# Reciprocal products of attention's first chunks on GpSimd, and feed-forward weights loaded inside the attention stage

## The chip, the cores and the metric

One core of a Trainium2 chip runs the whole program. The time is device microseconds of one execution; the median of several is compared. The program has four stages behind one another, each with its own instruction streams for TensorE (PE), VectorE (DVE), ScalarE (ACT), GpSimd (POOL) and SyncE (SP, which issues transfers). The streams run by themselves and meet only at semaphores and at the barrier between two stages.

## The reference

```python
# x: (4, 256, 56, 56)
x = x + conv(group_norm(x))           # 7x7 pairwise self-attention convolution, softmax over 49 taps
t = tokens(x)                         # (4, 3136, 256)
n = layernorm(t)
q, k, v = heads(n @ qkv_w.T + qkv_b)  # 8 heads of 32
s = (q @ k.T * 32**-0.5 + 5) ** 2
t = t + (s / s.sum(-1)) @ v @ proj_w.T + proj_b
n = layernorm(t)
w = n @ wr + br                       # one weight per token
sel = top(w, 3136 // 2 - 1)           # 1567 tokens of each batch
y = n
y[sel] += w[sel] * (gelu(n[sel] @ w1 + b1) @ w2 + b2)   # 256 -> 1024 -> 256
t = t + y
```

## The kernel before

The first two stages (group norm, projections and the convolution) run until about 1635 us and are not touched. The third is attention, the fourth the routed feed-forward.

**Attention.** A batch is `t`, 128 partitions x 2 x 3136 (channels on partitions, tokens along the free axis), in seven chunks of 448 tokens. `EARLY` is 5. Before the loop over the batches the first five chunks of batch 0 are normalized. For each chunk VectorE adds the input and the convolution's output into `t` (`residual`, line 1880, two inputs from SBUF); ScalarE squares (`square`, 1003); GpSimd adds the two halves of the sum and of the squares (`half_sum` 1008, `half_sq` 1013); PE averages over the channels with a matrix of 1/256 (`stats`, 1016, once for the mean and once for the squares); ScalarE squares the mean (`mean2`, 1037); VectorE takes the variance (1043) and subtracts the mean into `xn` (1048); ScalarE takes the square root (`std`, 1058); VectorE takes the reciprocal (1064) and multiplies `xn` by it (`scale`, 1068). The order on VectorE is, for chunk c: variance, subtraction, reciprocal, product, and the residual of chunk c + 2. ScalarE squares the residual of chunk c + 1 before the mean of chunk c. The last of the five chunks has its reciprocal and product later, beside the keys.

Behind the five chunks VectorE copies the selector matrix `sel` (2069), PE multiplies the value bias by the output projection (`pb_mm`, 2266), VectorE adds that to `pb_s` (2071), and then the loop over the batches begins with the key projections (PE 2127) and VectorE's addition of the key bias (1911). The loop runs three times, the fourth batch has a body of its own; for batches 1 to 3 the first five chunks are normalized beside the outputs of the batch before, by `center` and `scale`.

**The last batch's outputs.** For every chunk and each of two halves PE projects (2084) into PSUM and VectorE joins it with `t` into the single output tile `tout` (1886, semaphore `t2_done`); SP stores the tile (1678, `t2_out`), and the next chunk's join waits for that. Beside this the front of the feed-forward works: token tiles of batches 0 and 1 are turned (PE 1420) and their moments taken, batch 0's tokens are normalized, searched for the selected ones, scattered to DRAM by GpSimd (1218, 25 transfers) and the selected rows loaded back packed, by GpSimd's queue (1231, 1233, into `xc0`). SP's last instructions wait for all seven chunks' stores; then comes the barrier (1449).

**Routed feed-forward.** It allocates what remains of SBUF after the attention stage's buffers are given back, among them the weights `w1_s`, `w2_s`, `b1_s` and three tiles `tb` for adding back. GpSimd first issues the three loads of weights (2416, 1 MB for each matrix, 4 KB for the bias), then clears the end of `hid` (2417) and the last rows of `xc` (2418), then normalizes every second token tile of batch 1 (1215). PE turns four packed tiles (2589), which ScalarE copies (2484) once those clears are done, and then waits for the weights (`w_in`). After that every engine follows a list of positions written out by hand (`STEPS`): 32 up products (2599) and 13 down products (2609) for each batch, with the search, turning and normalizing of the next batches and the adding back of the last between them. ScalarE takes the square root of batch 1's variances (`root`, 1279) before its first gelu (2489).

## Time and profile before

| what | value |
|---|---|
| median of 3 runs | 3521.96 us (3514.76 to 3528.95) |
| the profiled execution | 3520.25 us |
| its span | 3518.4 us |
| PE busy | 3016.6 us, 86% |
| VectorE busy | 2481.0 us, 71% |
| GpSimd busy | 2145.4 us, 61% |
| ScalarE busy | 1981.1 us, 56% |
| granted TensorE clock, mean | 0.942 of full |

The page gives for each engine the sum of its instructions' times. The timeline gives start and length of each; in brackets stands the idle time before it and what ended that. An instruction's length runs from its start to its end, standing still for a port or a queue included.

### The profile page before, as it was taken

The page shows a single profiled execution, that of the slowest core. Times are in us where ns is not written, and L with a number is a line of the kernel's source. Part 1 is how long each engine was busy: PE and PEld are TensorE (multiplying, and loading weights), DVE is VectorE, ACT ScalarE, POOL GpSimd, SP SyncE. Part 2 cuts the span into 40 slices and gives each one's busy share as a digit, 9 for nine tenths or more (in the row PEclk, how much of TensorE's full clock was granted, in tenths as well). Part 3 has the DMA queues.
Part 4 walks back from the last instruction along what each step waited for, and adds up shares of the span by engine and source line. Part 5 has one row for each costly group of instructions (what it writes and reads, how often), then busy time and mean ns, then how long its engine had stood idle before and what let it go on. Part 6 is the DMA issues. An engine that isn't in the chain of part 4 may idle for free. (4 is left out here: it accounts for less than half of the span.)

```text
span 3518.4 us, 102494 instructions
## 1 busy us (share of the span) xinstructions
PE 3016.6 (86%) x42638; PEld 1526.2 (43%) x42638; DVE 2481.0 (71%) x2173; ACT 1981.1 (56%) x3387; POOL 2145.4 (61%) x1235
## 2 busy tenths in 40 slices
PE   4988888888888887875899999999999989689997
PEld 1234434444444443432552354335334533267775
DVE  6369999999999999997763676476558655364322
ACT  1566556666655666642458656865775576434221
POOL 3369988889999888975671177037505751234433
PEclk9999899988999998988899999999999999799998
DMA  6531111221212122103011211111111122235544
GB/s 227 159 122 59 58 52 36 65 62 55 63 50 62 36 65 60 57 16 105 13 54 36 67 29 42 46 54 29 54 54 33 30 57 75 105 114 174 161 146 146
DMA packets 190699, 257.34 MB, mean 73 GB/s; under 512 B 88974, under 2 KB 151674, under 8 KB 188216
## 3 DMA queue, kind: packets, MB, share of 16 engines
q1 hardware_dynamic: 178348, 218.25, 20.6%
q0 software_dynamic: 11520, 32.55, 3.0%
q8 instruction: 357, 5.85, 0.7%
q14 instruction: 78, 0.64, 0.1%
q10 hardware_dynamic: 396, 0.05, 0.0%
HBM read 152.23 MB, written 79.27 MB: 66 GB/s over the span
## 5 line engine op out<-in xcount | busy, mean ns | idle before, releaser
L847 PE MATMUL ps<-late,ident 32*32 32x504 f32 x21952 | 1097.2, 645 | 213.8 <-issue 143.9
L689 DVE TENSOR_TENSOR late<-ps,late 128x3584 f32<-128x3584 f32 x280 | 1056.4, 3792 | 103.4 <-PE ps L847 95.0
L847 PEld LDWEIGHTS ps<-late,ident 32*32 32x32 f32 x21952 | 485.0, 108 | 471.7 <-issue 402.0
L319 POOL TENSOR_TENSOR late<-ex,late 128x1792 f32<-128x1792 f32 x140 | 530.0, 3786 | 64.0 <-PE ps L847 31.2
L1583 POOL TENSOR_TENSOR pool<-share 128x768 f32<-128x768 f32 (+1 forms) x200 | 348.3, 1748 | 182.8 <-ACT share L1779 135.7
L1825 ACT ACTIVATE phq<-ps 128x896 f32<-128x896 f32 x448 | 391.9, 920 | 72.8 <-PE ps L2177 68.7
L287 POOL TENSOR_TENSOR y<-xa 128x1568 f32<-128x1568 f32 x98 | 324.2, 3316 | 116.8 <-PE ps L823 115.8
L298 POOL TENSOR_TENSOR ex<-lg,mx 128x1568 f32<-128x1568 f32 x98 | 345.7, 3546 | 12.7 <-DVE mx L670 12.7
L2177 PE MATMUL ps<-qst,sel 96*128 96x448 bf16 x1120 | 296.3, 357 | 22.2 <-ACT phq L1825 16.4
L519 ACT ACTIVATE ps<-ex 128x448 f32<-128x448 f32 x280 | 149.4, 534 | 284.8 <-DVE late L689 284.7
L1928 DVE TENSOR_TENSOR pool<-ps,share 128x1280 f32<-128x1280 f32 (+1 forms) x200 | 295.5, 1481 | 4.0 <-ACT ps L1785 2.8
L2150 PE MATMUL ps<-pool,share 128*32 128x288 f32 (+3 forms) x3200 | 236.8, 412 | 27.5 <-ACT pool L1790 12.7
L543 ACT ACTIVATE y<-ps,u2c,s2c 128x784 f32<-128x784 f32 x189 | 189.3, 1001 | 126.0 <-PE ps L823 125.7
L818 PE MATMUL ps<-y,cw1bd 32*32 32x392 f32 x3136 | 217.1, 518 | 20.8 <-ACT y L532 9.6
L2127 PE MATMUL ps<-share,xt 128*128 128x256 f32 (+1 forms) x800 | 225.1, 406 | 6.5 <-ACT share L1786 5.5
L2177 PEld LDWEIGHTS ps<-qst,sel 96*128 96x128 bf16 x1120 | 82.8, 98 | 320.2 <-ACT phq L1825 172.8
L550 ACT ACTIVATE lg<-ps,par 128x784 f32<-128x784 f32 x196 | 179.1, 914 | 75.4 <-PE ps L834 75.2
L2046 DVE TENSOR_TENSOR at<-ps,rd 128x448 f32<-128x448 f32 x56 | 35.0, 624 | 260.1 <-PE ps L2242 238.1
L1008 POOL TENSOR_TENSOR lm20a<-t 128x448 f32<-128x448 f32 x16 | 18.2, 1138 | 325.4 <-DVE t L1880 325.4
L834 PE MATMUL ps<-y,cw2bd 32*32 32x392 f32 x3024 | 186.5, 523 | 28.1 <-ACT y L543 23.1
L655 DVE TENSOR_TENSOR run<-lg,run 128x1568 f32<-128x1568 f32 x70 | 195.6, 2794 | 2.2 <-issue 1.6
L2599 PE MATMUL ps<-xct,w_s 128*128 128x392 f32 x512 | 181.0, 499 | 11.2 <-DMA w_s<-in_w 6.8
(280 smaller groups left out, 5029.0 us busy)
## 6 DMA issues: line engine op xcount, KB each, us to landing
late<-planes SPq DMA_DIRECT2D x14, 2480.0 KB, 9.0
pf<-pf_dram SPq DMA_DIRECT2D x392, 55.1 KB
planes<-ex SPq DMA_DIRECT2D x7, 1984.0 KB, 9.4
conv_dram<-late SPq DMA_DIRECT2D x56, 224.0 KB, 4.8
t<-in_x SPq DMA_DIRECT2D x28, 448.0 KB, 4.0
xt<-conv_dram SPq DMA_DIRECT2D x28, 448.0 KB, 6.3
t_dram<-tout SPq DMA_DIRECT2D x28, 448.0 KB, 2.9
pool<-t_dram SPq DMA_DIRECT2D x24, 512.0 KB
```

Source lines behind the costliest of these rows:

```text
L287: pool.tensor_tensor(o, x1, x2, ALU.subtract).then_inc(z_ready, 1)
L298: pool.tensor_tensor(ex[:, i], lg[:, i], m, ALU.subtract).then_inc(shifted, 1)
L319: pool.tensor_tensor(o[:, :, 0:SHARE], w.unsqueeze(2).broadcast_to([P, RW, SHARE, W]), xw, ALU.mult).then_inc(own_ready, 1)
L689: v.tensor_tensor(o, w, xw, ALU.mult).then_inc(prod_ready, 1)
L818: pe.matmul(ps[at:at + 32, k + r // 2, 0:CW].rearrange("p (j w) -> p j w", w=W), diag(cw1, r), y[32 * r:32 * r + 32, :, h * W:(h + 1) * W] ...
L847: mm = pe.matmul(ps[32 * h:32 * h + 32, 4 + r, 0:DENC], diag(ident, r), x[32 * r:32 * r + 32, h].rearrange("p s w -> p (s w)"), start=begi ...
L1583: pool.tensor_tensor(phk[j % 2][0:r, :, ROT_V * DH:FLIN].rearrange("p h (r i) -> p h r i", i=DH), ki.unsqueeze(2).broadcast_to([r, HPG, RO ...
L1825: act.activation(dst, src, ACT.Square).then_inc(phq_done, 1)
L1928: v.tensor_tensor(phk[j % 2][0:r, :, DH:ROT_V * DH].rearrange("p h (r i) -> p h r i", i=DH), same.unsqueeze(2).broadcast_to([r, HPG, ROT_V ...
L2127: mm = pe.matmul(ps[0:r, 4 + j % 2, 0:HPG * DH + P], xn[:, k, j * P:j * P + r], wkv_s[:, k, hg, :], start=(k == 0), stop=(k == CH - 1))
L2150: pe.matmul(ps[DH * h:DH * h + DH, f, 0:hi - lo], kv[j % 3][0:r, v0:v0 + DH], phk[j % 2][0:r, h, lo:hi], start=(j == 0), stop=(j == NT - 1))
L2177: mm = pe.matmul(ps[:, h, 0:CT], sel[:, f, :], qst[:, h, ch(c)], start=True, stop=True)
```

## The change

`scale` is split. In the chunks before the loop VectorE does only the reciprocal (`rstd`), and a new `scale_pool` has GpSimd multiply chunk c - 1 after the half sums of chunk c; the keys wait for these products. The last reciprocal there is followed by the selector's copy and the bias addition, which now stand before the variance of chunk 4, and PE does the bias product ahead of the averages of chunk 4. `t` belongs to `Front` and stays allocated in the feed-forward stage. `w1_s` and `w2_s` lie over its first 2048 columns, and two of the three `tb` tiles behind them. GpSimd issues the three loads inside the attention stage, once ten joins of the last batch are done (chunks 0 to 4, `WEIGHTS_FROM` is 5), ahead of the loads of packed rows. The wait for the last chunk's store moves from SP at the end of attention to SP and ScalarE in the feed-forward stage.

```diff
--- before.py
+++ after.py
@@ -1057,11 +1057,21 @@
         v = self.var[c % 2][:]
         act.activation(v, v, ACT.Sqrt, bias=self.eps[:]).then_inc(self.s_std_done, 1)
 
+    def rstd(self, v, n, c):
+        v.wait_ge(self.s_std_done, n * NCT + c + 1)
+        r = self.var[c % 2]
+        v.reciprocal(r[:], r[:]).then_inc(self.s_rstd, 1)
+
+    def scale_pool(self, pool, c):
+        pool.wait_ge(self.s_rstd, c + 1)
+        pool.wait_ge(self.s_cent, c + 1)
+        o = self.xn[:, :, self.ch(c)]
+        pool.tensor_tensor(o, o, self.var[c % 2][:].unsqueeze(1).broadcast_to([P, CH, CT]), ALU.mult).then_inc(self.s_xn_done, 1)
+
     def scale(self, v, n, c):
         i = n * NCT + c
-        v.wait_ge(self.s_std_done, i + 1)
+        self.rstd(v, n, c)
         r = self.var[c % 2]
-        v.reciprocal(r[:], r[:]).then_inc(self.s_rstd, 1)
         v.wait_ge(self.s_rstd, i + 1)
         v.wait_ge(self.s_cent, i + 1)
         o = self.xn[:, :, self.ch(c)]
@@ -1091,6 +1101,7 @@
 NEXT_TOK = [21 + p for p in range(NPAIR)]
 NEXT_MOMENTS = [range(0, 0)] * 5 + [range(0, 4), range(4, 8)]
 WIDEN_AT, SPREAD_AT, ROWS_AT = 6, 12, 14
+WEIGHTS_FROM = -(-CH * HID // CT)
 TURN = ((4, 5), (7, 6))
 
 
@@ -1110,7 +1121,7 @@
 
 
 
-    def __init__(self, ctx, nc, t2_dram, wr, br, b2, tri_dram, keep):
+    def __init__(self, ctx, nc, t2_dram, wr, br, b2, tri_dram, w1, b1, w2, keep):
         def sb(name, shape, dt=F32):
             return ctx.enter_context(nc.sbuf_tensor(name, shape, dt))
 
@@ -1119,6 +1130,7 @@
 
         self.ps = keep["ps"]
         self.sources = (wr, b2, br, tri_dram)
+        self.wide_sources = (b1, w1, w2)
         first = sb("xt0", [P, NT, CW1])
         self.xt = [first]
         self.xn = first[:].rearrange("p j c -> p (j c)")[:, 0:CH * S].rearrange("p (k s) -> p k s", s=S)
@@ -1150,6 +1162,12 @@
         self.yg03 = self.share[:, (NSEL_T + NT) * CW1:(NSEL_T + NT + 1) * CW1]
         self.ident = sb("ident2", [P, P])
         self.eps = sb("eps3", [P, 1])
+        self.t = sb("t", [P, CH, S])
+        low, high = self.t[:, 0], self.t[:, 1]
+        self.w1_s = low[:, 0:CH * HID].rearrange("p (k h) -> p k h", h=HID)
+        self.w2_s = high[:, 0:HT * C].rearrange("p (h c) -> p h c", c=C)
+        self.tb = [x[:, CH * HID:CH * HID + CH * GCOL].rearrange("p (k s) -> p k s", s=GCOL) for x in (low, high)]
+        self.b1_s = sb("b1_s", [P, HT])
         self.stat = rest(NT, 6)
         self.msum, self.mdif, self.var, self.rstd, self.nbias = [rest(NT) for _ in range(5)]
         self.key, self.res, self.low, self.high = [rest(NT) for _ in range(4)]
@@ -1167,6 +1185,8 @@
         self.seq_i, self.digit_i = self.sign, self.part[:, 0, 0:BASE - 1]
 
         self.first_in = sem("first_in3")
+        self.w_in = sem("w_in3")
+        self.t2_last = sem("t2_last")
         self.ready0 = sem("ready3")
         self.t_in = [sem(f"t_in{k}") for k in range(RING)]
         self.turned = sem("turned3")
@@ -1205,6 +1225,10 @@
         pool.iota(self.seq_i[:], [[P, NT]], base=1, channel_multiplier=1).then_inc(self.ready0, 1)
         pool.iota(self.digit_i, [[1, BASE - 1]], base=1, channel_multiplier=0).then_inc(self.ready0, 1)
         pool.memset(self.ones[:], 1.0).then_inc(self.ready0, 1)
+
+    def weights(self, pool):
+        for o, src in zip((self.b1_s, self.w1_s, self.w2_s), self.wide_sources):
+            pool.dma_start(o[:], src).then_inc(self.w_in, 16)
 
     def clear(self, pool):
         pool.memset(self.zeros[:], 0.0).then_inc(self.ready0, 1)
@@ -1454,7 +1478,7 @@
             return ctx.enter_context(nc.semaphore(name))
 
         ps = keep["ps"]
-        t = sb("t", [P, CH, S])
+        t = front.t
         xn = front.xn
         qsp = front.share[:, 0:3 * S // 2].bitcast(BF16).rearrange("p (f s) -> p f s", f=3)
         shared = [3 * S // 2]
@@ -1508,7 +1532,7 @@
         ready0 = sem("ready0")
         gate = sem("gate2")
         x_in = [sem(f"x_in2{c}") for c in range(NCT)]
-        t2_out = [sem(f"t2_out{c}") for c in range(NCT)]
+        t2_out = [sem(f"t2_out{c}") for c in range(NCT - 1)] + [front.t2_last]
         tsum = sem("tsum")
         pb_mm = sem("pb_mm")
         pb_done = sem("pb_done")
@@ -1619,6 +1643,8 @@
             for c in range(EARLY):
                 norm.half_sum(pool, tsum, 0, c)
                 norm.half_sq(pool, 0, c)
+                if c > 0:
+                    norm.scale_pool(pool, c - 1)
             pool.wait_ge(ready0, 7)
             with pool.Fori(0, B - 1) as b:
                 keys(b, 0)
@@ -1643,6 +1669,8 @@
             pool.wait_ge(front.placed, 1)
             for j in range(NT):
                 front.scatter_one(pool, 0, j)
+            pool.wait_ge(t2_done, (B - 1) * NCT * CH + WEIGHTS_FROM * CH)
+            front.weights(pool)
             pool.wait_ge(qst_in, 16 * 3 * HPG * B * NCT)
             pool.wait_ge(qst_last, 16 * 3 * HPG * B)
             pool.memset(front.xc0[:, NSEL_T - 1, :], 0.0).then_inc(front.ready0, 1)
@@ -1729,7 +1757,7 @@
                 front.load(sp, 1, g)
             for c in range(4, NCT):
                 store(B - 1, c)
-            for c in range(NCT):
+            for c in range(NCT - 1):
                 sp.wait_ge(t2_out[c], 16 * B)
 
         @block.scalar
@@ -2061,15 +2089,17 @@
             for c in range(EARLY):
                 norm.center(v, 0, c)
                 if c < EARLY - 1:
-                    norm.scale(v, 0, c)
+                    norm.rstd(v, 0, c)
                 if c + 2 < EARLY:
                     residual(0, c + 2)
-            v.wait_ge(w_in, NW_IN)
-            v.wait_ge(ready0, 7)
-            v.tensor_copy(sel[:], self32).then_inc(ready0, 1)
-            v.wait_ge(pb_mm, 1)
-            v.tensor_tensor(pb_s[:], pb_s[:], ps[:, 0, 0:CH], ALU.add).then_inc(pb_done, 1)
+                if c == EARLY - 2:
+                    v.wait_ge(w_in, NW_IN)
+                    v.wait_ge(ready0, 7)
+                    v.tensor_copy(sel[:], self32).then_inc(ready0, 1)
+                    v.wait_ge(pb_mm, 1)
+                    v.tensor_tensor(pb_s[:], pb_s[:], ps[:, 0, 0:CH], ALU.add).then_inc(pb_done, 1)
             v.wait_ge(pb_done, 1)
+            v.wait_ge(norm.s_xn_done, EARLY - 1)
             with v.Fori(0, B - 1) as b:
                 body(b, True)
             body(B - 1, False)
@@ -2258,13 +2288,14 @@
 
             pe.wait_ge(avg_in, 16)
             for c in range(EARLY):
+                if c == EARLY - 1:
+                    pe.wait_ge(w_in, NW_IN)
+                    for h in range(CH):
+                        for k in range(HG):
+                            mm = pe.matmul(ps[:, 0, h:h + 1], pw_s[:, k, h * P:(h + 1) * P], bv_s[:, k:k + 1], start=(k == 0), stop=(k == HG - 1))
+                    mm.then_inc(pb_mm, 1)
                 norm.stats(pe, 0, c)
-            pe.wait_ge(w_in, NW_IN)
             pe.wait_ge(ready0, 8)
-            for h in range(CH):
-                for k in range(HG):
-                    mm = pe.matmul(ps[:, 0, h:h + 1], pw_s[:, k, h * P:(h + 1) * P], bv_s[:, k:k + 1], start=(k == 0), stop=(k == HG - 1))
-            mm.then_inc(pb_mm, 1)
             pe.wait_ge(pb_done, 1)
             with pe.Fori(0, B - 1) as b:
                 body(b, True)
@@ -2329,21 +2360,18 @@
             return ctx.enter_context(nc.semaphore(name))
 
         ps = keep["ps"]
-        front = Front(ctx, nc, t2_dram, wr, br, b2, tri_dram, keep)
+        front = Front(ctx, nc, t2_dram, wr, br, b2, tri_dram, w1, b1, w2, keep)
         rows_dram = front.rows_dram = [nc.dram_tensor(f"rows_dram{b}", (ROWS, CW1), F32, kind="Internal").ap() for b in range(B)]
         attention_block(nc, front, *keep["attention"], keep)
 
-        tb = [sb(f"tb{k}", [P, CH, GCOL]) for k in range(RING)]
+        tb = front.tb + [sb("tb2", [P, CH, GCOL])]
         xt, dest, rows, ident = front.xt, front.dest, front.rows, front.ident
         yg = [front.yg + [front.yg03]] + [[sb(f"yg{k}{i}", [P, CW1]) for i in range(GT)] for k in range(1, RING)]
         xc = [front.xc0, sb("xc1", [P, NSEL_T, CW1])]
         xct = sb("xct", [P, CH, NUP])
         hid = sb("hid6", [P, HT, NSEL_T * P])
         yt = front.yt
-        w1_s = sb("w1_s", [P, CH, HID])
-        w2_s = sb("w2_s", [P, HT, C])
-        b1_s = sb("b1_s", [P, HT])
-        w_in = sem("w_in3")
+        w1_s, w2_s, b1_s, w_in = front.w1_s, front.w2_s, front.b1_s, front.w_in
         ready0, turned, placed = front.ready0, front.turned, front.placed
         tb_in = [sem(f"tb_in{k}") for k in range(RING)]
         out_st = [sem(f"out_st{k}") for k in range(RING)]
@@ -2412,8 +2440,6 @@
                             at += 1
                         tile += k
 
-            for o, src in ((b1_s, b1), (w1_s, w1), (w2_s, w2)):
-                pool.dma_start(o[:], src).then_inc(w_in, 16)
             pool.memset(hid[:, :, NUP:NSEL_T * P], 0.0).then_inc(ready0, 1)
             pool.memset(xc[1][:, NSEL_T - 1, :], 0.0).then_inc(ready0, 1)
             for j in range(1, NT, 2):
@@ -2452,6 +2478,7 @@
                 c0, w = q * GCOL, group_cols(q)
                 sp.dma_start(out_v[b, :, :, c0:c0 + w], tb[n % RING][:, :, 0:w]).then_inc(out_st[n % RING], 16)
 
+            sp.wait_ge(front.t2_last, 16 * B)
             for b in range(B + 1):
                 for pos, (kind, m, h) in enumerate(STEPS):
                     for q in range(NG):
@@ -2494,6 +2521,7 @@
                 pack(0, m)
             front.root(act, 1)
             act.wait_ge(w_in, NW_IN)
+            act.wait_ge(front.t2_last, 16 * B)
             for b in range(B):
                 for pos, (kind, m, h) in enumerate(STEPS):
                     if kind == "up":
```

## Rows read from the trace of the kernel before

**Rows 1.** The page's busy times: engine, us, share of the span, instructions.
```profile
PE 3016.6 (86%) x42638; PEld 1526.2 (43%) x42638; DVE 2481.0 (71%) x2173; ACT 1981.1 (56%) x3387; POOL 2145.4 (61%) x1235
```

**Rows 2.** The chain of waits in order of time: start us, us, what.
```profile
3047.78 0.58 POOL b_s L2416
...
3048.88 9.89 DMA w_s<-in_w
3058.81 2.98 PE ps L2599 x4
```

**Rows 3.** Timeline, start of attention, one chunk's period: start us, us, engine, line, operation.
```profile
1666.38 0.62 DVE L1043 TENSOR_TENSOR lvar0a<-ps,lm20a 128x448 f32<-128x448 f32 x1 [1.50 <-issue]
...
1667.91 2.95 DVE L1064 RECIPROCAL lvar0a<-lvar0a 128x448 f32<-128x448 f32 x1
...
1670.89 1.09 DVE L1068 TENSOR_TENSOR xt<-xt,lvar0a 128x896 f32<-128x896 f32 x1
1671.90 1.08 DVE L1880 TENSOR_TENSOR t<-t,xt 128x896 f32<-128x896 f32 x1
...
1674.49 0.62 DVE L1043 TENSOR_TENSOR lvar1a<-ps,lm21a 128x448 f32<-128x448 f32 x1 [1.50 <-issue]
```

**Rows 4.** Timeline, the end of the first chunks.
```profile
1677.84 1.70 PE L1016 MATMUL ps<-pool,avg 128*128 128x448 f32 x2
...
1680.02 0.62 DVE L1043 TENSOR_TENSOR lvar0a<-ps,lm20a 128x448 f32<-128x448 f32 x1
1680.55 1.08 DVE L1048 TENSOR_TENSOR xt<-t,ps 128x896 f32<-128x896 f32 x1
...
1681.55 0.48 DVE L2069 CAST sel<-share 96x640 bf16<-96x640 f32 x1
...
1682.17 1.84 PE L2266 MATMUL ps<-bv_s,pw_s 128*128 128x1 f32 x8 [2.64 <-DVE sel L2069]
...
1684.45 5.48 PE L2127 MATMUL ps<-share,xt 128*128 128x256 f32 x12 [0.44 <-DVE pb_s L2071]
1686.56 0.29 DVE L1911 TENSOR_TENSOR share<-ps,share 128x128 f32<-128x128 f32 x1 [2.35 <-PE ps L2127]
```

**Rows 5.** Timeline, VectorE and GpSimd at once: convolution, then start of attention.
```profile
698.88 2.58 DVE L655 TENSOR_TENSOR run<-lg,run 128x1568 f32<-128x1568 f32 x1
699.73 1.96 POOL L320 COPY late<-ex 128x224 f32<-128x224 f32 x1
...
1646.15 1.13 POOL L1013 TENSOR_TENSOR pool<-pool 128x448 f32<-128x448 f32 x1
1646.28 1.96 DVE L1880 TENSOR_TENSOR t<-t,xt 128x896 f32<-128x896 f32 x1 [1.29 <-DMA xt<-conv_dram]
...
1697.79 1.74 POOL L1583 TENSOR_TENSOR pool<-share 128x768 f32<-128x768 f32 x1
```

**Rows 6.** Timeline, end of attention and start of the feed-forward.
```profile
3035.51 9.11 SPq L1678 DMA_DIRECT2D t_dram<-tout  x2
...
3043.54 0.68 DVE L1886 SCALAR_TENSOR_TENSOR tout<-ps,pb_s,t 128x448 f32<-128x448 f32 x1 [1.93 <-PE ps L2084]
...
3047.36 1.09 PE L2589 MATMUL ps<-ident,share 128*128 128x128 f32 x4 [3.87 <-PEq L1449]
...
3050.07 0.34 POOL L2418 MEMSET xc<- 128x257 f32 x1
...
3051.60 0.81 ACT L2484 ACTIVATE xct<-ps 128x256 f32<-128x256 f32 x2 [0.51 <-PE ps L2589]
```

**Rows 7.** Joins before the end; transfers of 3003 to 3030 (last: us to landing); a window.
```profile
3018.29 0.69 DVE L1886 SCALAR_TENSOR_TENSOR tout<-ps,pb_s,t 128x448 f32<-128x448 f32 x1 [3.11 <-PE ps L2084]
...
3028.38 0.69 DVE L1886 SCALAR_TENSOR_TENSOR tout<-ps,pb_s,t 128x448 f32<-128x448 f32 x1 [0.53 <-PE ps L2084]
...
t_dram<-tout SPq DMA_DIRECT2D x1, 448.0 KB, 2.8
...
3052.00:3059.00 7.00, 0.19 (x1) 0.19 (x2) 0.50 (x2) 0.59 (x2) 5.71 (x11) 0.50 0.87 362
```

## The prediction

> **What bounds the kernel now.** I read the page's totals first: PE is busy for 86% of the span [rows 1], so no engine idles for long and gains can only come from seams. Then the chain of waits: through the feed-forward stage it is almost all matmuls, and its first long piece is a transfer, 9.89 us of weights at 3048.88, behind three issues on GpSimd, and the first feed-forward matmul stands at 3058.81 when it lands [rows 2]. That is one seam. The other is the start of attention, read from the timeline: PE works there only in snatches, because five chunks of batch 0 are normalized one after another and VectorE carries the chain [rows 3], with the bias product after them [rows 4]. Batches 1 to 3 are normalized beside other work, and the loop's code is not touched, so the two seams are all that can move.
>
> **Part A, the first chunks. Period of a chunk.** From one variance to the next VectorE takes 1674.49 - 1666.38 = 8.11 us [rows 3]: variance and subtraction, the reciprocal (2.95, starting at 1667.91), the product (1670.89), the residual of the chunk after next (1671.90), ending 1672.98, and 1.51 us in which ScalarE squares that residual and then the mean. The change takes the product out. What it occupied is 1671.90 - 1670.89 = 1.01 us, plus the gap behind the reciprocal: the product waited for the reciprocal's own semaphore (1670.89 against an end at 1670.86), while an instruction without such a wait starts about 0.08 us before its forerunner ends (1671.90 against 1671.98). So 1.09 us a chunk go, for the three chunks 0 to 2 behind whose reciprocal a residual stands: 3.3 us.
>
> **What GpSimd does with the product.** It costs more there: 128x768 took 1.74 us [rows 5]; scaled to 128x896 that is an estimate of 2.05. GpSimd is idle at that moment, and nobody waits for these products before the keys begin. But its queue is in order: the next chunk's two half sums stand behind the product. And the two engines do not run freely side by side. A residual (two inputs from SBUF, 1.08 us elsewhere) that began at 1646.28, with GpSimd on a half product since 1646.15, took 1.96 us: it ended 0.96 us after GpSimd did. The other way round, a GpSimd copy begun at 699.73 while VectorE had run a two-input operation since 698.88 took 1.96 us and ended 0.23 after it [rows 5]. So whoever starts first keeps the other out. After the change the product (released by the reciprocal's semaphore, some 0.08 us after its end) and the residual (not waiting for it, 0.05 to 0.08 before that end) meet at every chunk. I take VectorE as first, by about 0.15 us: the residual costs its 1.08, GpSimd stands for 1.0 and multiplies for 2.05, so it is free 2.15 us after the residual, and the half sums (1.13 each) end 4.4 us after it. PE's averages need those and the subtraction before them, which ends 3.1 us after the residual; the first half sum is there at 3.3. PE starts 0.1 to 0.2 late and has 2 us to spare before the next variance. So the price on the path is nothing; if GpSimd is first, it is 2.0 us a chunk.
>
> The Trainium skill (SBUF — State Buffer, section "SBUF: two separate sides") says the same of the pair: an exclusive lock, held for the whole instruction by whichever starts first, between GpSimd and a VectorE operation with two SBUF inputs. By that rule alone either order is possible, and the second is a rival below.
>
> **The end of the prologue.** Call the last chunk-3 variance V (1674.49 now). Now: the last averages end at V + 5.05 (1677.84 + 1.70), but VectorE still multiplies, so the variance of chunk 4 starts at V + 5.53 (1680.02), its subtraction 1680.55, the copy of the selector 1681.55, then PE's bias product (1682.17, 1.84 us), its addition, the first projection at V + 9.96 (1684.45) and VectorE's first key addition at V + 12.07 (1686.56) [rows 4]. After: the bias product stands on PE ahead of the last averages, in a hole that PE has there (its chunk-3 averages end 5 us after the variance before, the period is 7.0, the product takes 1.8; the small weights have landed, DMA was idle from about 1665, some 4 us before). The reciprocal of chunk 3 ends at V + 4.48, the copy (0.48) and the addition follow, the variance of chunk 4 starts at about V + 5.25, the subtraction ends at V + 6.9; GpSimd's last product, held off by the copy if by anything, ends at V + 7.1. PE may project from V + 5.5, the first projection takes the 2.1 us that it takes now, so the first key addition starts at V + 7.6 instead of V + 12.07. That is 4.45 us. Part A: 3.3 + 4.45 = 7.75 us. If the averages or the entry of the loop are a little later, 6.5; at most 8.5.
>
> **Part B, the seam before the feed-forward.** First, the stage ends earlier. Now SP waits for the last output store: issued by 3044.62 (the second of the two from 3035.51), landed 2.3 us later, and PE starts at 3047.33 to 3047.36 [rows 6]. After, nothing waits for it at the barrier; the last to arrive is SP with its issue at 3044.62, or VectorE at 3044.22 (3043.54 + 0.68). With the same 0.45 us of barrier the stage starts at 3045.1: 2.25 us. ScalarE and SP wait for that store later, at about 3046.9, before anything they need.
>
> Second, GpSimd no longer issues three loads, 1.62 us from 3047.78 [rows 2], ahead of the two clears. ScalarE's copies of the turned rows wait for the second clear. Now clear at 3050.07, second pair of copies ending 3052.41 (3051.60 + 0.81): 2.34 us [rows 6]. After: GpSimd starts 0.45 after the stage does, clears hid (0.7), the second clear starts at 3046.2, the copies end at 3048.6. Then nothing holds the first feed-forward matmul but these copies, for the weights are there: it starts at 3048.6 instead of 3058.81, 10.2 us in all, the 2.25 among them. ScalarE's square root of the second batch's variances waits for VectorE until about 3049.1, still ahead of the first gelu (the first up product needs 3.0 us [rows 2], PE being granted half its clock there [rows 7]). What follows (gelu, normalizing, the second search) is engine work that starts behind that matmul and moves with it.
>
> **Are the weights there?** They are issued once the tenth output tile of the last batch is joined: 3018.29 + 0.68 = 3019.0 [rows 7]. Beside the tokens' loads, 3.5 MB moved in 9.9 us now, at 362 GB/s [rows 2, 7]. After, 2.1 MB of weights and then the packed rows (1.57 MB, whose issue is now behind that wait on GpSimd's queue instead of at 3004) take an estimated 10 to 12 us at such a rate and are there by 3033, with 12 us to spare. They run beside one output store, whose landing (2.8 us now) frees the single output tile for the join at 3028.38; it is issued at about 3020 and so may take 8 us. I take nothing for it; bounds -0 and +2 us.
>
> **Sum.** 7.75 + 10.2 = 17.95 us. The profiled execution took 3520.25 (span 3518.4), so 3502.3 by it. The median of the three runs is 1.7 above it: 3504.0 for a median.
>
> **Rivals.**
> (1) GpSimd takes the port first. For: the instruction that lost in [rows 5] came only 0.13 us late, and my lead for VectorE is no larger. Against: a semaphore lies between on GpSimd's side, none on VectorE's. Then the residual ends 3.1 us after the reciprocal instead of 2.1 as now; each of three chunks gets 1.0 longer instead of 1.1 shorter, and the selector's copy waits for the last product too (1.6 of the 4.45 lost): A becomes about -3 + 2.9, nothing. 10.2 us remain: 3511.8. The Trainium skill's rule on the pair, above, allows this.
> (2) The weights are early but another wait takes their place: the packed rows, the root, the second batch's normalizing on ScalarE, or the averages. Half of B's second piece gone: about 13 us gained, 3509.
> (3) Slower: the copies crowd the output stores. Place: the store of chunk 4 and the join at 3028.38, then everything behind. If 3.7 MB moved at 73 GB/s, the page's mean over the span, and ahead of the store, they would take 50 us, and the joins and with them the stage would move by X, up to 42. It decides from X = 17.95, where the store lands 26 us after 3020. At X = 36 the time is 3540. Against: 362 GB/s just there, and DMA otherwise idle from 3023 to 3036.
> (4) More: PE keeps its upper clock over the shorter pause. The first four up matmuls take 2.98 us, against 1.32 later; 1.7 to 2 us more, 3502.
>
> **Numbers.** Forecast 0.55, rival (1) 0.19, (2) 0.15, (3) 0.03, (4) 0.08. Half a per cent, about what a measurement of this kernel tells from no change (its three runs lie 0.4% apart), is 17.6 us, so the forecast lies on the boundary: slightly under half of it, (4), and some scatter of the runs make 0.42 for faster; within 0.5%, 0.55; slower 0.03. The range reaches from the forecast with its upper bounds and (4), less a scatter of the runs, 3496, to (1) with scatter, 3514.
>
> **What would show it.** The reciprocals' period on VectorE at the start: 7.0 us right, 9.1 rival (1), where the residuals would last 3 us and not 1.1. GpSimd's products would show as 3 us long, standing first. First key addition 7.75 earlier against the stage's first residual. PE's first up matmul 3.5 us behind the stage's first transposition (now 11.5). Output joins at the same distances as now: otherwise (3). Wrong altogether if the chunks' period is unchanged, or the up matmul waits for a transfer.

## The result

| what | before | changed |
|---|---|---|
| median, 7 runs each | 3517.91 us (3510.69 to 3528.95) | 3493.71 us (3489.99 to 3502.16) |
| ratio | 1 | 0.9934 (0.9922 to 0.9946) |
| profiled execution | 3520.25 us | 3502.16 us |
| its span | 3518.4 us | 3500.1 us |
| granted TensorE clock, mean | 0.942 | 0.945 |

The change is faster by 0.66%, with 24.2 us between the medians. The two traces lie 18.3 us apart. The forecast was 3504.0 for a median of runs, 17.95 us of gain, range 3496 to 3514: the time lies 2.3 us below the range. Two further measurements of the same program gave ratios of 0.9951 and 0.9939, with 20.3 and 20.5 us between the medians (below).

The start of attention in the changed kernel, from its timeline, against [rows 3] and [rows 4] (line 1063 is the reciprocal now, 1069 GpSimd's product, 1908 the residual, 1939 the key addition):

```profile
1665.88 0.63 DVE L1043 TENSOR_TENSOR lvar0a<-ps,lm20a 128x448 f32<-128x448 f32 x1 [1.51 <-issue]
...
1667.41 2.94 DVE L1063 RECIPROCAL lvar0a<-lvar0a 128x448 f32<-128x448 f32 x1
...
1670.28 1.03 DVE L1908 TENSOR_TENSOR t<-t,xt 128x896 f32<-128x896 f32 x1
1670.44 2.81 POOL L1069 TENSOR_TENSOR xt<-xt,lvar0a 128x896 f32<-128x896 f32 x1 [1.95 <-DVE lvar0a L1063]
1670.72 1.38 PE L2295 MATMUL ps<-bv_s,pw_s 128*128 128x1 f32 x8
...
1672.81 0.62 DVE L1043 TENSOR_TENSOR lvar1a<-ps,lm21a 128x448 f32<-128x448 f32 x1 [1.50 <-issue]
...
1677.21 0.43 DVE L2098 CAST sel<-share 96x640 bf16<-96x640 f32 x1
1677.37 2.21 POOL L1069 TENSOR_TENSOR xt<-xt,lvar1a 128x896 f32<-128x896 f32 x1 [1.94 <-DVE lvar1a L1063]
...
1677.61 0.62 DVE L1043 TENSOR_TENSOR lvar0a<-ps,lm20a 128x448 f32<-128x448 f32 x1
1678.14 4.67 PE L2157 MATMUL ps<-share,xt 128*128 128x256 f32 x12 [0.76 <-DVE pb_s L2100]
...
1680.24 0.29 DVE L1939 TENSOR_TENSOR share<-ps,share 128x128 f32<-128x128 f32 x1 [1.02 <-PE ps L2157]
```

A chunk's period is 1672.81 - 1665.88 = 6.93 us (8.11 before). The residual starts 0.16 us before GpSimd's product and keeps its 1.03 us. The product is 2.81 us long: for 0.87 of them the residual still runs, and the product ends 1.94 after it. The bias product lies in PE's hole. With V for the start of chunk 3's variance (1672.81 here), the last variance starts at V + 4.80 and the key addition at V + 7.43.

The seam before the feed-forward, same timeline, against [rows 6] and [rows 7]:

```profile
3010.61 0.68 DVE L1914 SCALAR_TENSOR_TENSOR tout<-ps,pb_s,t 128x448 f32<-128x448 f32 x1 [3.10 <-PE ps L2114]
...
3012.19 1.11 POOL L1231 DMA_DIRECT2D t<-in_w  x2
...
3020.70 0.68 DVE L1914 SCALAR_TENSOR_TENSOR tout<-ps,pb_s,t 128x448 f32<-128x448 f32 x1 [0.53 <-PE ps L2114]
...
3035.85 0.68 DVE L1914 SCALAR_TENSOR_TENSOR tout<-ps,pb_s,t 128x448 f32<-128x448 f32 x1 [1.93 <-PE ps L2114]
3037.58 0.74 POOL L2443 MEMSET hid<- 128x768 f32 x1 [22.05 <-POOLq L1473]
...
3037.61 0.63 PE L2617 MATMUL ps<-ident,share 128*128 128x128 f32 x4 [1.80 <-PEq L1473]
3038.25 0.31 POOL L2444 MEMSET xc<- 128x257 f32 x1
...
3039.04 0.71 PE L2617 MATMUL ps<-ident,share 128*128 128x128 f32 x4 [0.80 <-ACT xct L2511]
...
3039.52 0.66 ACT L2511 ACTIVATE xct<-ps 128x256 f32<-128x256 f32 x2 [0.26 <-PE ps L2617]
3040.32 2.93 PE L2627 MATMUL ps<-xct,t 128*128 128x392 f32 x4 [0.57 <-ACT xct L2511]
```

The stage starts 1.08 us after the last join's end (3.14 before), and the first up matmul 2.71 us after that (11.45 before): it waits for ScalarE's copy and no longer for a transfer. The joins at 3010.61 and 3020.70 are 10.09 us apart, as 3018.29 and 3028.38 were: the weights' transfers do not hold up the store between them.

The table cuts the span at the same four events in two traces of the kernel before and three of the changed one, so that the scatter can be seen too (us):

| stretch | before | before, again | changed | changed, again | changed, third |
|---|---|---|---|---|---|
| start to first residual | 1643.89 | 1636.69 | 1645.76 | 1638.75 | 1642.74 |
| first residual to first key addition | 42.67 | 41.84 | 34.48 | 34.46 | 34.11 |
| first key addition to last join's end | 1357.66 | 1355.31 | 1356.29 | 1354.23 | 1332.12 |
| last join's end to first up matmul | 14.59 | 14.64 | 3.79 | 3.79 | 3.78 |
| first up matmul to the end | 459.59 | 458.32 | 459.78 | 460.37 | 457.75 |

The seams (the second and the fourth stretch) gained 8.19 and 10.80, together 18.99 us, between the first two traces, and 7.38 and 10.85, together 18.23, between the second two. The first seam depends a little on the clock that PE is granted: in the second trace of the kernel before, the bias product of [rows 4] runs at the upper level (1.00) and takes 1.02 us instead of 1.84 (at 0.50):

```profile
1674.96 1.02 PE L2266 MATMUL ps<-bv_s,pw_s 128*128 128x1 f32 x8 [2.64 <-DVE sel L2069]
```

The other three stretches changed by +1.87, -1.37 and +0.19 between the first two traces. That is less than two traces of one program differ by: 7 us in the untouched first stages, and 2.4 in the loop.

### The profile page after: what moved, and what is told of

Same layout as the page of the kernel before. It is cut to its first block and busy times, and to the rows that moved or that the text cites. A ratio compares the mean times of both kernels' runs of the same rounds, so it can differ in the third digit from the quotient of the medians.

```text
span 3500.1 us, 102496 instructions
## 1 busy us (share of the span) xinstructions
PE 3013.7 (86%) x42638; PEld 1522.5 (43%) x42638; DVE 2473.5 (71%) x2169; ACT 1982.7 (57%) x3387; POOL 2161.7 (62%) x1239
## 5 line engine op out<-in xcount | busy, mean ns | idle before, releaser
L2180 PE MATMUL ps<-pool,share 128*32 128x288 f32 (+3 forms) x3200 | 237.0, 412 | 27.3 <-ACT pool L1818 13.5
L818 PE MATMUL ps<-y,cw1bd 32*32 32x392 f32 x3136 | 220.4, 525 | 21.9 <-ACT y L532 10.2
L1008 POOL TENSOR_TENSOR lm20a<-t 128x448 f32<-128x448 f32 x16 | 18.2, 1137 | 314.3 <-DVE t L1908 314.3
L2637 PE MATMUL ps<-t,hid 128*128 128x256 f32 x832 | 187.5, 382 | 0.0
```

Of the source, the lines that this page charges most:

```text
L2180: pe.matmul(ps[DH * h:DH * h + DH, f, 0:hi - lo], kv[j % 3][0:r, v0:v0 + DH], phk[j % 2][0:r, h, lo:hi], start=(j == 0), stop=(j == NT - 1))
L2637: mm = pe.matmul(ps[:, 2 + n % 2, 0:C], hid[:, k, m * P:(m + 1) * P], w2_s[:, k, :], start=(k == 0), stop=(k == HT - 1))
```

## The experiments

The diffs are against the changed kernel, where nothing else is said.

**The change again, and the kernel before against itself** (no edit), both on one chip with the next two.

> The changed kernel as it is, measured once more. The two profiled executions differ by 18.3 us, the medians of seven runs by 24.2 (ratio 0.9934, 0.9922 to 0.9946). Theory S (the seams): the gain is the two seams' 8.2 and 10.8 us, 19.0 in all, ratio 0.9946, and what the runs showed beyond it is scatter of the stages that were not touched; a second trace shows the same two seams within 0.3 us, and other stretches that differ by some us either way. Theory X (more than the seams): the gain is 24 us, ratio 0.993, and the second trace has some 5 us in a stretch outside the seams that both traces of the kernel before lack.

> The kernel before, measured against itself, as a scale for all others. Theory S: ratio 1.000, its interval reaching 0.1% to either side; its second trace differs from the first by some us in the convolution, nothing at the seams (first residual to first key addition 42.7 us; last join's end to first up matmul 14.6). Theory X: the same ratio, and the two traces agree to 1 us in every stretch, so that a surplus of 5 us can't be scatter.

Measured: the change 3496.33 us against 3516.6 (29 runs of before), ratio 0.9951 (0.9935 to 0.9968); before 3516.24, ratio 1.0009 (0.9996 to 1.0021). The seams are the table's. The traces bear out theory S: no stretch outside the seams is shorter in both of these traces of the change than in both of before. What the first seven runs gained beyond 19 us is not in any trace.

**Each half by itself.** The first has, on the kernel before, only the new `rstd`, `scale_pool`, and the orders at the start of attention:

```diff
-                    norm.scale(v, 0, c)
+                    norm.rstd(v, 0, c)
...
+                if c > 0:
+                    norm.scale_pool(pool, c - 1)
```

the second, on the kernel before, only the weights over `t` and the moved wait:

```diff
-            for c in range(NCT):
+            for c in range(NCT - 1):
                 sp.wait_ge(t2_out[c], 16 * B)
...
+            pool.wait_ge(t2_done, (B - 1) * NCT * CH + WEIGHTS_FROM * CH)
+            front.weights(pool)
```

> Only the start of attention is changed: products of chunks 0 to 3 on GpSimd, selector copy, bias product and its addition ahead of the last variance and averages. The weights are loaded where they were. Theory S: 8.2 us gained, ratio 0.9977; first residual to first key addition 34.5 us instead of 42.7, chunk period 6.9. Theory X: 8 to 13 us, if the surplus hangs on this part.

> Only the seam before the feed-forward is changed: weights over the dead rows beside the last outputs, last store not waited for at the barrier. The start of attention is as before. Theory S: 10.8 us gained, ratio 0.9969; last join's end to first up matmul 3.8 us instead of 14.6. Theory X: 11 to 16 us, if the surplus hangs on this part (three large tiles fewer in the last stage, other addresses).

Measured for the first half: 3505.96 us, ratio 0.9975 (0.9964 to 0.9986), first seam 34.11, the other 14.79. For the second: 3504.04, ratio 0.9961 (0.9948 to 0.9974), first seam 42.67, the other 3.79. The halves are independent: each seam is as in the whole change or as before. By the ratios they gain 8.8 and 13.7 us, and each interval holds its seam's gain.

**GpSimd made first.** VectorE waits for the semaphore that releases GpSimd's product, and clears three small tiles, before its residual.

```diff
                 if c + 2 < EARLY:
+                    v.wait_ge(norm.s_rstd, c + 1)
+                    for k in range(3):
+                        v.memset(corr[k][:], 0.0)
                     residual(0, c + 2)
```

> The changed kernel, but before each of the three residuals that follow a reciprocal VectorE waits for the reciprocal's semaphore and clears three columns of 32, so that GpSimd's product is under way when the residual starts. Theory L (whoever starts first keeps the other out for its whole instruction): the residuals take 2.8 to 3.0 us instead of 1.03, GpSimd's products 1.9 instead of 2.8, the chunk period is 8.9 instead of 6.93, first residual to first key addition 40.5 instead of 34.5: 6 us lost. Theory P (the two share the bandwidth): residual and product both lengthen by some tenths, period 7.2 to 7.5, 35.5 from end to end, 1 us lost.

Measured: 3477.05 us against 3493.55 beside it, ratio 0.9948 (0.9928 to 0.9968); 40.56 us from first residual to first key addition, chunk periods 9.47, 9.08 and 9.08. Its timeline:

```profile
1661.28 0.17 DVE L2096 MEMSET corr<- 128x32 f32 x3
1661.29 2.07 POOL L1069 TENSOR_TENSOR xt<-xt,lvar1a 128x896 f32<-128x896 f32 x1 [3.78 <-DVE lvar1a L1063]
1661.37 2.94 DVE L1908 TENSOR_TENSOR t<-t,xt 128x896 f32<-128x896 f32 x1
```

The residual came 0.08 us after the product and ends 0.95 us after it: it takes 2.94 us instead of 1.03, while the product needs 2.07, undisturbed. This is theory L, within 0.2 us in every figure; under theory P both would have become longer by tenths. So the exclusion of the forecast's rival (1) is real: the residual that starts 0.16 us first gives a period of 6.9 us, the one that starts 0.08 us late one of 9.1. (Some 0.2 us of the difference is the added wait and clearing.) The runs alone do not tell this kernel from the change (0.9939 for that on the same chip); the timeline does. In the changed kernel VectorE was first at all three chunks in all its traces (periods 7.33, 6.93 and 6.93).

**The bias product sooner, alone** (on the kernel before; products stay on VectorE).

```diff
+                if c == EARLY - 2:
+                    v.wait_ge(w_in, NW_IN)
+                    v.wait_ge(ready0, 7)
+                    v.tensor_copy(sel[:], self32).then_inc(ready0, 1)
...
+                if c == EARLY - 1:
+                    pe.wait_ge(w_in, NW_IN)
```

> Of the change only the order at the end of the first chunks: selector copy, bias product and addition ahead of the last variance and averages. Products on VectorE, weights loaded where they were. Theory S (the parts add up): chunk periods as before (8.5, 8.1, 8.1), last chunk-3 variance to first key addition 8.5 us instead of 12.1, so 3.6 of the 8.2 us come from here and 4.6 from the products. Rival: without the product moved VectorE is the later one at the end and little is gained, 1 us at most, since PE has to wait for the addition anyway.

Measured: 3488.07 us, ratio 0.9979 (0.9967 to 0.9991); periods 8.52, 8.11, 8.11, and 38.18 us from first residual to first key addition.

```profile
1681.94 1.09 DVE L1068 TENSOR_TENSOR xt<-xt,lvar1a 128x896 f32<-128x896 f32 x1
1682.94 0.48 DVE L2070 CAST sel<-share 96x640 bf16<-96x640 f32 x1
...
1683.84 1.99 PE L2128 MATMUL ps<-share,xt 128*128 128x256 f32 x8 [1.57 <-DVE pb_s L2072]
...
1685.01 0.29 DVE L1911 TENSOR_TENSOR share<-ps,share 128x128 f32<-128x128 f32 x1
```

The key addition stands directly behind VectorE's subtraction, no longer behind PE, whose first two projections took 1.99 us (granted clock 1.00; in [rows 4] three took 5.48 at 0.50). What the order is worth depends on the trace of before that one compares with: 42.67 - 38.18 = 4.5 us where the bias product ran at the lower clock, 41.84 - 38.18 = 3.7 where it ran at the upper. The next experiment, whose start of attention is that of before, has 41.83 on this chip, which speaks for 3.7, as expected. The products then bring the rest: 38.18 - 34.11 = 4.1 us against the traces of the change whose first projections ran mostly at the upper clock, 3.7 against 34.48, where they ran at the lower.

**The weights early, the barrier late** (on the kernel before, the second half alone, with SP's wait for the last store left where it was; the diff shown is against the second half).

```diff
-            for c in range(NCT - 1):
+            for c in range(NCT):
                 sp.wait_ge(t2_out[c], 16 * B)
```

> Weights loaded over the dead rows, start of attention as before, but SP waits for all seven chunks' stores at the end of attention, as the kernel before does. Theory S: last join's end to the stage's start 3.1 us instead of 1.1, start to first up matmul 2.7 as in the whole change: 8.7 of the 10.8 us come from the weights and 2.1 from the barrier. Rival: the store's landing is only moved, and what waits for it later (SP's token loads, ScalarE) costs the 2 us there: then this kernel is as fast as the one with the early barrier, 10.8 us gained.

Measured: 3479.99 us, ratio 0.995 (0.9931 to 0.9969). Its timeline:

```profile
3016.11 0.68 DVE L1902 SCALAR_TENSOR_TENSOR tout<-ps,pb_s,t 128x448 f32<-128x448 f32 x1 [1.93 <-PE ps L2100]
...
3019.93 0.76 PE L2602 MATMUL ps<-ident,share 128*128 128x128 f32 x4 [3.87 <-PEq L1463]
...
3023.04 2.95 PE L2612 MATMUL ps<-xct,t 128*128 128x392 f32 x4 [0.56 <-ACT xct L2496]
```

The stage starts 3.14 us after the last join's end, the up matmul 3.11 after that: 6.25 against 3.79. So 8.4 us of the seam are the weights' and 2.5 the barrier's. That is 0.4 more than the 2.06 by which the stage starts later: the second pair of tiles is turned at a granted clock of 0.50 and takes 1.12 us, where the changed kernel has 1.00 and 0.71. The rival, that the moved wait costs the 2 us again later, is not borne out by the traces: SP's first load of the stage starts 3.16 us after the last join's end here and 2.63 in the changed kernel, and from the first up matmul to the end this trace has 458.16 us, inside the 457.75 to 460.37 of the change. The runs do not fit the seam so well: by the ratio of four runs the gain is 17.5 us, from 10.8 to 24.1, where the seam brings 8.4. No stretch of the trace shows the difference, and it stays open.

**The weights behind the last join.**

```diff
-WEIGHTS_FROM = -(-CH * HID // CT)
+WEIGHTS_FROM = -(-CH * HID // CT) + 2
```

> The changed kernel with the weights, and the packed rows behind them on GpSimd's queue, issued after all fourteen joins instead of ten: their whole transfer stands behind the last join. Theory D (3.7 MB at the rate of this queue decide): they land some 12 us after the last join, the first turned tile then, the first up matmul 14 to 16 us after the last join instead of 3.8; 11 us lost, and so the change has had 12 us or more of room, as forecast. Rival: the rows are there sooner than the weights since both move at once; the up matmul then waits for the weights alone, 10 to 11 us after the last join, 7 us lost.

Measured: 3487.17 us, ratio 0.9987 (0.9977 to 0.9996). Its timeline:

```profile
3002.56 0.69 DVE L1914 SCALAR_TENSOR_TENSOR tout<-ps,pb_s,t 128x448 f32<-128x448 f32 x1 [1.93 <-PE ps L2114]
...
3019.48 1.08 PE L2617 MATMUL ps<-ident,share 128*128 128x128 f32 x4 [16.96 <-PEq L1473]
...
3022.58 2.95 PE L2627 MATMUL ps<-xct,t 128*128 128x392 f32 x4 [0.56 <-ACT xct L2511]
```

and its barrier line, 1473, listed by sequencer (a drain is the instruction that each engine's program has ahead of its arrival at the barrier; length in ns, start in us), then the same in the changed kernel:

```profile
L1473 POOLq DRAIN  x1: 12891/12891/12891, 3006.3 to 3006.3; - x1
```

```profile
L1473 POOLq DRAIN  x1: 13731/13731/13731, 3014.4 to 3014.4; - x1
```

Both theories were too low: the up matmul comes 19.3 us after the last join's end, 15.5 later than in the change. The whole stage's start waits, not only PE: GpSimd's drain ends at 3019.2, some 2 us after the transfer engines fall idle (they moved 92 GB/s from 3016 to 3017 and 4 in the next microsecond), and the stage starts 0.3 us behind it. In the changed kernel that drain ends at 3028.1, 9.2 us before SP's, the last to come (3037.3). In its trace on the other chip it ends at 3005.5 and SP's comes at 3009.8, 4.3 us later. There GpSimd is still issuing scatters when the tenth join is done (2983.71), and so issues the weights only at 2989.13. The room is there, but smaller than the forecast's 12 us.

**The mean squared first,** a further step: ScalarE squares a chunk's mean before the next residual, and GpSimd's product stands one chunk later.

```diff
-                if c > 0:
-                    norm.scale_pool(pool, c - 1)
+                if c > 1:
+                    norm.scale_pool(pool, c - 2)
+            norm.scale_pool(pool, EARLY - 2)
...
+            square(0, 1)
             for c in range(EARLY):
-                if c + 1 < EARLY:
-                    square(0, c + 1)
                 norm.mean2(act, 0, c)
+                if 0 < c < EARLY - 1:
+                    square(0, c + 1)
                 norm.std(act, 0, c)
```

> A further step on the changed kernel. ScalarE squares the mean of chunk c before it squares the residual of chunk c + 1, so that the next variance needn't wait for that residual's square, and GpSimd adds the half sums of chunk c before its product of chunk c - 2. Theory V (VectorE's own instructions are the chain then): period 5.4 to 5.5 us instead of 6.93, first residual to first key addition 30.0 instead of 34.5, 4.4 us faster than the change, ratio 0.993 to the kernel before. Rival E (PE's averages or the port decide): averages that start behind the half sums hold the variances at a period of 6.5 to 6.8, or products that reach into the next residual lengthen it by up to 2 us; then 33.5 or more, no gain that can be measured.

Measured: 3467.44 us against 3493.55, ratio 0.9919 (0.9902 to 0.9937); 29.73 us between the two events. Its timeline:

```profile
1658.52 0.61 DVE L1043 TENSOR_TENSOR lvar0a<-ps,lm20a 128x448 f32<-128x448 f32 x1
1658.64 0.95 ACT L1003 ACTIVATE pool<-t 128x896 f32<-128x896 f32 x1 [1.47 <-DVE t L1910]
...
1660.86 2.08 POOL L1069 TENSOR_TENSOR xt<-xt,lvar1a 128x896 f32<-128x896 f32 x1
...
1663.05 1.03 DVE L1910 TENSOR_TENSOR t<-t,xt 128x896 f32<-128x896 f32 x1
1663.99 0.61 DVE L1043 TENSOR_TENSOR lvar1a<-ps,lm21a 128x448 f32<-128x448 f32 x1
```

The variance follows the residual without a gap, the period is 5.47 us, and GpSimd's product ends at 1662.94, 0.11 us before the residual that it would hold up. That is theory V.

**It and the change side by side.** (no further edit)

> The version with the mean squared first, against the change on the same chip. From the first trace of it (period 5.47, 29.7 us from first residual to first key addition): 4.7 us faster than the change, ratio to the kernel before 0.9933 by the seams alone; and the median 4 to 6 us under that of the change beside it. If it were only scatter, the two medians would lie within 2 us of each other in either order.

> The changed kernel once more, beside the next three on one chip. Theory S (the two seams, 19.0 us): ratio 0.9946 (0.9935 to 0.9957), seams 34.5 and 3.8 us again. Theory X (24 us or more): ratio 0.993. If the attention loop has no stall during the 25 scatters here (1330 us between first key addition and last join instead of 1354 to 1358), the kernel before lacks it too and the ratio stays.

Measured: 3467.78 us, ratio 0.9926 (0.9911 to 0.9941), 29.73 us again; the change 3472.12 us, ratio 0.9939 (0.9923 to 0.9955). The medians are 4.3 us apart, the seams 4.4 (34.11 against 29.73). This version clearly beats the kernel before. Against the change the traces show 4.4 us, twice; the intervals of the runs overlap, so they agree with it but do not show it by themselves.

**The scatters held back.**

```diff
             pool.wait_ge(front.placed, 1)
+            pool.wait_ge(t2_done, (B - 1) * NCT * CH + 3 * CH)
```

> The changed kernel with GpSimd's 25 scatters of batch 0 held until the third chunk of the last batch is joined, about 45 us later. It bears on a stall of 22 to 26 us that six traces of the kernels show while these scatters are issued (all engines stand, released by nothing the profile shows) and four traces, all taken on one chip, don't. Theory I (the scatters' traffic holds up something that every engine needs): on a chip with the stall it moves with the scatters, to 2990 and later. Theory N (it belongs to that place in the engines' programs): it stays at 2955 to 2985, without any scatter beside it. On a chip without it both expect nothing; the packed rows land before the stage ends and the time is that of the change within 1 us.

Measured: 3471.45 us, ratio 0.994 (0.9925 to 0.9955). This was a miss: the sixth join ends at 2948.88 and the first scatter is issued at 2955.02, so the wait held nothing, and the chip was the one without the stall (described in the last section). It counts as one more measurement of the change and says nothing about the stall.

## Why the prediction was right or wrong

*The chunk period.* Right: 1.09 us were to go, 1.18 went (7.0 forecast, 6.93 measured). The forecast's own rows give 1.12 and not 1.09 (1671.90 less 1670.86 - 0.08), and the residual became 0.05 shorter, 1.03 for 1.08.

*Who has the port.* Right, and the step most at risk: VectorE was first, by 0.16 us where 0.15 was argued, and GpSimd stood for 0.87 where 1.0 was. The product's own length was an estimate of 2.05 us and is 2.07. The experiment shows the rival's price as forecast, 2.15 us a chunk for 2.0. The Trainium skill (SBUF — State Buffer, section "SBUF: two separate sides") has the rule, that whichever of the two starts first keeps the other out for its whole instruction, and the traces agree in both orders.

*The end of the prologue.* Right in mechanism, 0.17 us too late (V + 7.43 for V + 7.6, so 4.64 us for 4.45). With the three periods' 3.54 for 3.3 the first seam brought 8.19 for 7.75, within its 6.5 to 8.5.

*The seam before the feed-forward.* The earlier barrier brought 2.06 us for 2.25. On the weights the forecast was right: the up matmul waits for ScalarE's copies alone, 2.71 us after the stage's start where 3.5 was forecast. Two things make the 0.8. GpSimd's clears start with the stage (3037.58) and not 0.45 us behind it, as its first issue of weights did before. And the second pair of tiles is turned in 0.71 us in every trace whose stage starts 1.08 us after the last join, and in 1.11 or 1.12 in every other. That is the small part of rival (4) that happened; the first pair took anything from 0.63 to 1.09 us after the same longer pause, and the up matmul itself still took 2.93. Together the seam brought 10.80 for 10.2.

*Room for the transfers.* There was enough, but the account of it was incomplete. Not only PE would have waited for a late transfer: GpSimd's drain would have held the barrier. And the estimate of 10 to 12 us was too short: from the issue at 3011.59 the transfer engines were busy until about 3025, 13.5 us, and the drain ended after 16.5.

*The sum.* 17.95 forecast, 18.99 by the seams of the first two traces. The two seams were the right mechanism, and their size was off by 1.04 us.

*The level.* Here the prediction failed, in the step from the gain to a time and a range: "The median of the three runs is 1.7 above it: 3504.0 for a median", and the lower end, "less a scatter of the runs, 3496". That end is the forecast less 2.75 for the upper bounds and (4), less some 5 us for the scatter. The median of those three runs was 3521.96; of seven runs it is 3517.91, and of 29 on another occasion 3516.6. So of the 10.3 us between forecast and time, 4.05 are the base, 1.04 the seams, and 5.2 are in neither. No trace shows the 5.2; the two later measurements, with 20.3 and 20.5 us between the medians, speak for scatter of the runs, and 20.5 off the base of 3517.91 would have been inside the range. What the runs showed in place of the 5 us: the three runs of the base lay 14 us apart, and two traces of one program differ by 11.6 us in span (3518.4 and 3506.8). That the profiled execution came out at 3502.16 for the 3502.3 forecast is luck, by the same figures.

*The chances.* 0.42 for faster by over 0.5% was fair for a gain of 18 us, at the boundary. Four measurements of this program (the last with its idle wait) give 0.9934, 0.9951, 0.9939 and 0.9940; weighted by their intervals that is 0.9940, or 21 us with about 2.5 to either side. The seams' 19.0 is inside, their 18.2 of the second two traces just outside. The same holds more widely: of the twelve ratios of changed kernels here, eleven show more than their seams, ten by 0.4 to 5.3 us and one by 8 (those of one occasion share their runs of before, so they are not independent). Whether a part of that is real is open: no trace shows it.

## What to carry to other kernels

Before VectorE's work is given to GpSimd, see which instruction of VectorE with two inputs from SBUF meets it: the one of the two that starts first keeps its own length, the other waits for its partner's end, and here leads of 0.16 and 0.08 us decided. In a kernel whose engines are busy, look for the seams between stages: a load that stands behind a barrier can go over rows that nobody reads any more beside the last outputs, if it is issued early enough for the drain at the barrier. A forecast of a time needs the scatter of the base in its range, not only that of the gain.

## What the runs showed of the hardware

Two chips ran these kernels 23 us apart (medians of before 3516.6 and 3493.55), and the traces show the place. All four traces of the one have a stall of 26 us in the last batch, while GpSimd issues the 25 scatters, and so have the first two traces, before (22 us) and changed (26 us), whose chip is not on record. None of the eight traces on the other chip has it: there the stretch from first key addition to last join takes 1330 to 1333 us, and 1353 to 1358 in the six others. VectorE's row in the change's second trace, then a window of it and one of the mean-first version on the other chip, both amid the scatters (columns: window, length, busy us and count of PE, weight loads, VectorE, ScalarE, GpSimd, granted clock, DMA share, GB/s):

```profile
2987.94 0.62 DVE L2074 TENSOR_TENSOR at<-ps,rd 128x448 f32<-128x448 f32 x1 [26.32 <-remote]
```

```profile
2979.00:2988.00 9.00, 0.21 (x1) 0.00 (x0) 0.06 (x1) 0.06 (x1) 3.88 (x4) 0.50 0.24 87
```

```profile
2970.00:2982.00 12.00, 10.91 (x70) 4.75 (x70) 3.96 (x11) 8.94 (x13) 9.25 (x11) 1.00 0.57 186
```

In the first window PE, VectorE and ScalarE stand while GpSimd issues on and the transfer engines are three quarters idle; PE's granted clock there is 0.50, its lower level. What the engines lack is not in the profile, and the one attempt to move the stall held nothing, so the cause is open. It is larger than the whole change, but on that chip both kernels have it alike (26.28 us before, 26.32 changed), so that it leaves the ratio as it is.

GpSimd's drain at the barrier ended 1 to 3 us after the transfers of its own queue in four traces: 12.9 us long with the packed rows behind the last join, 13.7 and 13.0 in the changed kernel on the two chips, and 9.1 in the kernel before, where it had ended 34 us before the barrier opened and cost nothing. SP's drain took 0.007 us in each, so it does not wait in that way: in the changed kernel it came at 3037.3, while a store that SP had issued at 3036.56 landed 2.6 us after that. That GpSimd's waits for the landing is inferred from these times.
